# A graph-attention layer on one Trainium2 core: the setup phase reordered, with a second DMA queue on GpSimd

## What is computed

```python
# x [8192, 256], adj [8192, 8192] of zeros and ones, context [8192, 512], W_common [256, 512]
in_fts = context @ W_common.T
left  = in_fts @ w_left  + b_left
right = in_fts @ w_right + b_right
logits = left[:, None] + right[None, :]
logits = where(logits >= 0, logits, 0.2 * logits)
logits = where(adj <= 0, -inf, logits)
out = layernorm(x + relu(softmax(logits, axis=-1) @ x))
```

## Time and profile before

| | us |
|---|---|
| median of 3 runs | 1517.51 (1517.49 to 1521.56) |
| the profiled execution, time | 1518.96 |
| its span in the trace | 1517.2 |
| TensorE busy | 1385.1 (91%) |
| VectorE busy | 1317.8 (87%) |
| ScalarE busy | 645.2 (43%) |
| GpSimd busy | 88.8 (6%) |
| DMA | 329.59 MB, 217 GB/s on average |

### The profile page before, as it was taken

The page is one execution under the profiler, slowest core; times in us unless marked ns, Lnnn a source line. Parts: engine busy times, 40 slices in busy tenths (PEclk is TensorE's granted clock), DMA queues, the critical chain, the costliest instruction groups (busy, mean ns, idle before and its releaser), DMA issues.

```text
span 1517.2 us, 28376 instructions
## 1 busy us (share of the span) xinstructions
PE 1385.1 (91%) x12334; PEld 1207.3 (80%) x12334; DVE 1317.8 (87%) x1178; ACT 645.2 (43%) x690; POOL 88.8 (6%) x214
## 2 busy tenths in 40 slices
PE   1007699999999999999999999999999999999998
PEld 0005588888888888888888888888888888888887
DVE  6759899988998999989998989899998989899881
ACT  0194444443444444443444444344444444444430
POOL 0033000000000000000000000000000000000000
PEclk7558899999999999999999999999999999999999
DMA  9972998989889898989888898989889888988860
GB/s 386 336 167 78 224 234 210 241 213 233 218 220 224 209 230 211 239 215 232 220 218 223 213 225 214 233 220 233 220 219 226 212 225 215 231 217 219 209 168 11
DMA packets 86544, 329.59 MB, mean 217 GB/s; under 512 B 19728, under 2 KB 44304, under 8 KB 52624
## 3 DMA queue, kind: packets, MB, share of 16 engines
q1 hardware_dynamic: 81776, 321.47, 82.8%
q10 hardware_dynamic: 4640, 6.29, 1.5%
HBM read 319.29 MB, written 8.39 MB: 216 GB/s over the span
## 4 chain that ended last, share of the span: by engine, by line
PE 89%; DVE 4%; SPq 3%; DMA 2%; ACT 1%; issue 0%; POOL 0%; POOLq 0%; DVEq 0%
PE ps L352 30%; PE ps L349 30%; PE ps L350 29%; SPq L213 3%; DVE X L615 2%; DMA T<-in_x_dram 2%; DVE strip L652 1%; DVE T L696 1%; DVE tab L518 1%; DMA strip<-in_adj_dram 0%; PE ps L316 0%; ACT strip L423 0%; DMA wcol<-in_L_gnn_w_left_dram 0%; ACT X L394 0%; ACT gw L389 0%
## 5 line engine op out<-in xcount | busy, mean ns | idle before, releaser
L349 PE MATMUL ps<-X,T 128*128 128x257 f16 x4096 | 1117.5, 273 | 38.5 <-DVE T L696 38.4
L350 PE MATMUL ps<-X,T 128*128 128x257 f16 x4096 | 1114.6, 273 | 0.0
L352 PE MATMUL ps<-X,T 128*128 128x257 f16 x4032 | 1107.6, 275 | 0.0
L423 ACT ACTIVATE strip<-strip 128x2048 f32<-128x2048 f32 x256 | 489.2, 1911 | 505.7 <-DMA strip<-in_adj_dram 505.4
L696 DVE STREAM_TRANSPOSE T<-strip 128x2048 f32<-128x2048 f32 x256 | 588.8, 2301 | 74.3 <-PE ps L352 74.3
L652 DVE SCALAR_TENSOR_TENSOR strip<-tab,arow,strip 128x2048 f32<-128x2048 f32 x256 | 597.9, 2336 | 51.5 <-ACT strip L423 50.8
L349 PEld LDWEIGHTS ps<-X,T 128*128 128x128 f16 x4096 | 405.6, 99 | 91.9 <-issue 21.1
L350 PEld LDWEIGHTS ps<-X,T 128*128 128x128 f16 x4096 | 399.9, 98 | 60.8
L352 PEld LDWEIGHTS ps<-X,T 128*128 128x128 f16 x4032 | 391.1, 97 | 54.7
L404 ACT ACTIVATE xs<-ps,small 128x256 f32<-128x256 f32 x64 | 30.3, 473 | 158.2 <-DVE small L701 158.2
L304 POOL TENSOR_SCALAR small<-small 128x1 f32<-128x1 f32 x64 | 12.2, 190 | 1311.6 <-ACT xs L412 1311.6
(11 more groups left out here) (96 smaller groups left out, 250.7 us busy)
## 6 DMA issues: line engine op xcount, KB each, us to landing
strip<-in_adj_dram SPq DMA_DIRECT2D x1016, 256.0 KB, 4.7
xs<-in_L_gnn_context_dram SPq DMA_DIRECT2D x15, 1024.0 KB, 9.7
T<-in_L_gnn_context_dram SPq DMA_DIRECT2D x4, 2048.0 KB, 16.7
X<-in_L_gnn_context_dram SPq DMA_DIRECT2D x4, 2048.0 KB, 34.1
xs<-in_x_dram SPq DMA_DIRECT2D x64, 128.0 KB, 5.1
out_dram<-xs SPq DMA_DIRECT2D x64, 128.0 KB, 5.1
xs<-in_x_dram SPq DMA_DIRECT2D x4, 512.0 KB, 27.8
xs<-in_x_dram ACTq DMA_DIRECT2D x4, 512.0 KB, 20.0
```

Of the source, the lines that this page charges most:

```text
L349: nc.tensor.matmul(ps[o][:, 0:D + 1], hi, X16[:, jb, 0:D + 1], start=(i == 0), stop=False)
L350: nc.tensor.matmul(ps[o][:, 0:D + 1], lo, X16[:, jb, 0:D + 1], start=False, stop=False)
L352: m = nc.tensor.matmul(ps[o][:, 0:D + 1], hi, X16[:, jb, D + 2:2 * D + 3], start=False, stop=(i == JB - 1))
L423: nc.scalar.activation(s, s, ACT.Relu, scale=KEEP).then_inc(s_m, 1)
```

## The change

1. **Second queue.** ScalarE issues no DMA any more. GpSimd issues quarters 2 and 3 of strips 0 to 3 and of x, with semaphores of their own (`s_adjp`, `s_xq`), once the seventh context chunk has landed. SyncE issues quarters 0 and 1 of strips 0 to 3 ahead of those of x, and behind x the context rows of the second `left` block, into `gw`, where the first block's rows lay; the sums of squares write their unused result to PSUM in place of `gw`.
2. **Group 0 ahead of x.** ScalarE takes `keep` of strips 0 to 3, then the sums of squares. VectorE masks and transposes strips 0 to 3, and only then, at n = 4, runs the ones column and `x_factors`.
3. **Halves of x.** Blocks are taken from 63 down to 0. `NPL` is 12: 52 low parts are VectorE's, 13 ahead of each of `masked(4)` to `masked(7)`, and GpSimd makes its 12 (three pairs of operations) after VectorE's 52. ScalarE makes 13 high parts ahead of each of `keep(4)` to `keep(7)`, and the last 12 behind `keep(7)`.
4. **Around group 1.** `masked(8)` comes behind the transpose of strip 7. SyncE waits for the low parts behind the load of strip 11 in place of strip 7.
5. **Shorter chain to the tables.** The operations that prepared the general (wide-spread) case leave the path; the bias add is folded into scalars; ScalarE runs one exponential on a zero at the start.
6. **left steps.** Two operations fewer for each of 15 blocks.

```diff
@@ sync
-            sp.wait_ge(s_dot, 2 * CT)
-            for c in range(NX):
-                for q in (0, 1):
-                    x_quarter(sp, c, q)
             sp.wait_ge(s_v, 2)
             for n in range(NB):
                 for q in (0, 1):
                     strip_quarter(sp, n, q)
+            sp.wait_ge(s_dot, 2 * CT)
+            for c in range(NX):
+                for q in (0, 1):
+                    x_quarter(sp, c, q, s_x[c])
+            sp.wait_ge(s_ld, LB)
+            load_left_rows(1)
...
-                if n == NB - 1:
+                if n == 2 * NB - 1:
                     sp.wait_ge(s_xl, JB - NPL)
                     sp.wait_ge(s_xp, NPL)
-                    load_left_rows(1)
@@ gpsimd
+            pool.wait_ge(s_ctx[NCH - 2], 16)
+            pool.wait_ge(s_v, 2)
+            for n in range(NB):
+                for q in (2, 3):
+                    strip_quarter(nc.gpsimd, n, q, s_adjp[n])
+            pool.wait_ge(s_dot, 2 * CT)
+            for c in range(NX):
+                for q in (2, 3):
+                    x_quarter(nc.gpsimd, c, q, s_xq[c])
             pool.wait_ge(s_Fx, 1)
+            pool.wait_ge(s_xl, JB - NPL)
@@ scalar
-            act.wait_ge(s_ctx[NCH - 3], 16)
-            act.wait_ge(s_dot, 2 * CT)
-            for c in range(NX):
-                for q in (2, 3):
-                    x_quarter(nc.scalar, c, q)
-            act.wait_ge(s_v, 2)
-            for n in range(NB):
-                for q in (2, 3):
-                    strip_quarter(nc.scalar, n, q)
-            act.wait_ge(s_arg, 3)
+            act.wait_ge(s_one, 3)
+            nc.scalar.activation(warm, zero, ACT.Exp)
+            act.wait_ge(s_arg, 2)
...
             with act.If(general == 0):
+                for n in range(NB):
+                    keep(n)
                 for c in range(NX):
                     square_sums(c)
-                for n in range(NB):
-                    keep(n)
-                    for j in order[n * 6:n * 6 + 6]:
-                        high_part(j)
-                for j in order[NB * 6:JB // 2]:
-                    high_part(j)
...
+                    if n < 2 * NB:
+                        for j in order[(n - NB) * 13:(n - NB + 1) * 13]:
+                            high_part(j)
                     keep(n)
-                    if n < 2 * NB:
-                        for j in order[JB // 2 + (n - NB) * 8:JB // 2 + (n - NB + 1) * 8]:
+                    if n == 2 * NB - 1:
+                        for j in order[NB * 13:JB]:
                             high_part(j)
@@ vector
             with dve.If(general == 0):
-                x_factors()
                 masked(0)
                 for n in range(NS):
...
-                    if n + 1 < NS and not SG - 1 <= n < 2 * SG - 1:
+                    if n + 1 < NS and not SG - 1 <= n < 2 * SG:
                         masked(n + 1)
                     if n == SG:
+                        one_columns()
+                        x_factors()
                         dve.wait_ge(s_Fx, 1)
-                        part = (JB - NPL) // SG
                         for i in range(SG):
-                            for j in range(NPL + i * part, NPL + (i + 1) * part):
+                            for j in order[i * 13:(i + 1) * 13]:
                                 low_part(j)
                             masked(n + i)
                         dve.wait_ge(s_xl, JB - NPL)
                     transposed(n, n % NB, g, g % 2, k)
+                    if n == 2 * SG - 1:
+                        masked(n + 1)
```

More of the change, by code:

```diff
@@ L47, in build @@
     LW = LB * SG
-    NPL = 28
+    NPL = 12
     NHI = 2
@@ L117, in xrows @@
             return rows if n > 1 else rows.rearrange("p j d -> p (j d)")
[L119 to L122, removed]
+        order = list(range(JB - 1, -1, -1))
         when = {j: i for i, j in enumerate(order)}
         mx2, ssx = small[:, 0:2], small[:, 2:3]
-        rmin = small[:, 3:4]
         amx = small[:, 4:7]
-        spread, flag, flagf, fast, gscale, cap = (small[:, c:c + 1] for c in range(8, 14))
+        cap, flag, zero, warm = (small[:, c:c + 1] for c in range(8, 12))
         pe2, sc = small[:, 14:15], small[:, 15:16]
@@ L185, in build @@
         s_adj = [sem(f"adj_in{b}") for b in range(NB)]
+        s_adjp = [sem(f"adj_by_pool_in{b}") for b in range(NB)]
+        s_xq = [sem(f"x_by_pool_in{c}") for c in range(NX)]
         s_m = sem("mask_or_exponentials_ready")
@@ L477, in _ @@
                 general_steps(1)
-                with act.Fori(2, NG // NY - 1) as it:
+                with act.Fori(2, NG // NY) as it:
                     general_steps(it)
-                general_steps(NG // NY - 1, more=False)
             for g in range(NG - 2, NG):
@@ L578, in _, with table @@
-            dve.wait_ge(s_word, 6)
-            nc.vector.scalar_tensor_tensor(out=word[:, :], in0=word[:, :], scalar=fast, in1=gen[:, :],
-                                           op0=ALU.mult, op1=ALU.add).then_inc(s_word, 1)
-            dve.wait_ge(s_word, 7)
-            nc.vector.transpose(tab[:, :].rearrange("p (c j) -> p j c", c=B),
-                                word[:, 0:JB].rearrange("p (j c) -> p j c", c=1).broadcast_to([P, JB, B])).then_inc(s_tab, 1)
+            def table():
+                nc.vector.transpose(tab[:, :].rearrange("p (c j) -> p j c", c=B),
+                                    word[:, 0:JB].rearrange("p (j c) -> p j c", c=1).broadcast_to([P, JB, B])).then_inc(
+                    s_tab, 1)
@@ L593, in x_factors, with second_left_dots @@
+            def second_left_dots():
+                dve.wait_ge(s_lc, 32)
+                for q in range(LB):
+                    left_dot(1, q, lctx01, Xflat[:, q % 2 * CIN:(q % 2 + 1) * CIN])
+                    if q < LB - 1:
+                        dve.wait_ge(s_ld, LB + q)
+                left_by_strip(1)
             def x_factors():
@@ L616, in low_part, with general_tables, left_step @@
                                                in1=X16[:, j, 0:D], op0=ALU.mult, op1=ALU.subtract).then_inc(s_xl, 1)
-            def left_step(b, k):
+            def general_tables():
+                nc.vector.memset(F[:, :], 1.0).then_inc(s_gt, 1)
+                nc.vector.tensor_scalar(word[:, 0:JB], r[:, :], rmax, -1.0 / BIG, ALU.subtract, ALU.mult).then_inc(s_gt, 1)
+                dve.wait_ge(s_amx, 6)
+                nc.vector.tensor_scalar(arow[:, 0:LW], pt[:, 0:LW], c2, None, ALU.add).then_inc(s_gt, 1)
+                dve.wait_ge(s_gt, 3)
+                table()
+                dve.wait_ge(s_tab, 3)
+            def left_step(b, k, fast=True):
+                if not fast and isinstance(b, int) and b == 1 and k <= 11:
+                    return
                 if 7 <= k < 7 + LB:
@@ L623, in left_step @@
                     dve.wait_ge(s_ld, b * LB + q - 1)
-                    left_dot(b, q, lctx, ljunk[:, q % 2, :])
+                    left_dot(b, q, lctx01 if isinstance(b, int) and b == 1 else lctx, ljunk[:, q % 2, :])
                 if k == 11:
@@ L748, in _ @@
             with dve.Else():
+                second_left_dots()
+                general_tables()
+                one_columns()
                 x_factors()
                 dve.wait_ge(s_Fx, 1)
-                for j in range(NPL, JB):
+                for j in order[0:JB - NPL]:
                     low_part(j)
```

164 lines of the change are left out of this document (82 added, 82 removed).

## The result

| | before | after |
|---|---|---|
| median of 6 runs each, us | 1518.77 | 1512.16 (1510.99 to 1514.82) |
| the profiled execution's span, us | 1517.2 | 1509.6 |
| TensorE busy | 1385.1 | 1390.0 |
| first high part, H | 92.6 | 109.3 |
| group 1 starts | 163.3 | 152.1 |

The ratio is 0.9955 (95% interval 0.9945 to 0.9965): faster by 0.45%, some 7 us, where 23.3 us (to 1494.2) was forecast. The sign was right, the size off by a factor of more than three, and the time lies above the stated range, which ended at 1508.

What follows compares the result with a forecast made beforehand. TensorE's waits for VectorE's transposes before group 2 were taken as the bound. H at 96.5 plus 66.2 starts group 2 at 162.7 against 186.0, 23.3 us off, giving a median of 1494.2 us; range 1486 to 1508.

Steps and rivals of the forecast that it cites:

- When is H: End of setup: x lands at 91.6, two sums of squares follow, first high part at 96.5, 3.9 us later than before.
- both move at 348 GB/s while two queues run: Setup loads from about 52 us: SyncE's and GpSimd's queues together move x and strips at 348 GB/s.
- rivals 3 and 4: Setup: GpSimd issues at 10 to 15 ns a packet, 1499 to 1517, chance 0.12; 17 to 20 ns, 1526 to 1540, 0.08.
- GpSimd's last quarter of x by 92: Setup, sign to look for in GpSimd's queue: its last x quarter lands by 92 us.
- the 236 GB/s of the earlier trace: Setup loads: rate taken for one queue left alone, against 348 GB/s for two.
- The sums of squares: Setup on ScalarE: 16 of 1.18 us, 19 us from 67, ready at 86 and then waiting for x.
- Tables and group 0: Setup: table transpose near 63, strips 0 to 3 masked and transposed from 65 to 83, all covered by x's arrival.
- The ladder from H to group 1: First high part to group 1: transposes 4 to 7 end at H+40.6, GpSimd at H+42.4, group 1 starts at H+43.
- Group 2: Behind group 1: VectorE's transpose of strip 11 sets the start, H+66.2 = 162.7, against 186.0 before.
- The sum: Whole kernel: group 2 starts 23.3 us sooner, span 1517.2 becomes 1493.9, median forecast 1494.2 us.
- the rivals: Setup and feed: x sooner, 1486 to 1490, chance 0.18; later feed, 1499 to 1506, 0.15; slower GpSimd, 0.12 and 0.08.

Runs made afterwards that it cites:

- e9: Changed kernel with six of the 16 sums of squares moved from ScalarE to VectorE; 1510.86 us, ratio 0.9941.
- e10: e6 with six of the 16 sums of squares moved from ScalarE to VectorE; 1500.84 us, ratio 0.9870.
- e6: Changed kernel with SyncE's quarters of x read in 4 KB pieces in place of 1 KB; 1505.88 us, ratio 0.9910.
- e7: Changed kernel with GpSimd issuing only its strip quarters, and ScalarE issuing quarters 2 and 3 of x in portions between its work; 1509.67 us, ratio 0.9940.
- e8: e7 with ScalarE's last x transfers issued earlier and six of the 16 sums of squares on VectorE; 1501.00 us, ratio 0.9878.
- e1: Changed kernel with GpSimd's 18 transfers issued by ScalarE behind the same waits; 1510.39 us, ratio 0.9934.
- e3: Changed kernel with SyncE's quarters of x read in pieces of 8 to 16 KB in place of 1 KB; 1518.47 us, ratio 0.9987.

## Why the prediction was wrong

**When is H: wrong, and the main miss.** The failing step is "both move at 348 GB/s while two queues run". I took the pace of ScalarE's queue for GpSimd's, and asked of it only how fast it issues. It issues fast: 18 transfers in 10.3 us, from 43.7 to 54.0, while VectorE's dot products ran without a gap (busy 10.0 of the 10 us from 44 to 54), so rivals 3 and 4, with their ns a packet and the dot products that shut GpSimd out, were about the wrong quantity. The sign that I had named, GpSimd's last quarter of x by 92, came true (no packet of its queue moves after 90), and H was late all the same: it was SyncE's half that starved. What changed is the packet: 4640 for 6.29 MB became 1568 for the same bytes. Turns by packet then starve SyncE. Landing of the last chunk: 91.6 forecast, 105.1 in e9, 93.7 with packets alike (e10). The Trainium skill says it in "DMA: Bandwidth & Descriptors", "Queues, rings and completion order": each engine goes round between the queues a packet at a time. The traces bear this rule out: equal packet counts wherever both queues had work throughout the window. I weighed the same page for who writes the descriptors, and passed over this rule. I had also misread the 236 GB/s of the earlier trace rows as one queue left alone; it was two queues, SyncE's at 224 packets and ScalarE's at 77, which ran to 85 and not to 73.

**The sums of squares: wrong, hidden behind the first miss.** "Ready at 86 and wait for x" had the first chunk at 67. It lands at 74.5 to 78.7 even with like packets (e6, e7, e8, e10), and 19 us of sums stand behind it. In the changed kernel dividing the sums is worth 0 (e9); with like packets 2.4 to 5.8 us (e6 to e10, above).

**Tables and group 0: right.** Tables near 63 and at 62.2; strips from 65 to 83 in both. All of it lies ahead of the last sum of squares, at 107, so it delays nothing; what it gains is that these strips no longer stand in the ladder.

**The ladder from H to group 1: right to 0.2 us.** Forecast and trace: low parts 0.40 each; `masked(7)` H+31.7 and H+31.6; transposes H+40.6 and H+40.5; GpSimd H+42.4 and H+42.3; group 1 H+43 and H+42.8, at full clock.

**Group 2: right in kind, small in size.** Forecast H+66.2, started at H+67.7, and the low clock behind a wait of 3.2 us added the other 1.4: 2.9 us in all (1400.3 from H to the end, against 1397.4 forecast). What waited was not the first matmul of group 2 but the matmul of the left factors ahead of it; I had named VectorE's lateness and not priced the clock.

**The sum.** 12.8 us at H and 2.9 behind it are all of the 15.7 us by which 1509.6 exceeds 1493.9. Of the 12.8, like packets and divided sums together give back 11.2 (e10). The other 1.6 was not tested. One thing that the forecast had wrong is of this size: the strips moved at 282 GB/s and not at 348, although their packets were alike (129 and 127, 0.71 and 0.70 MB, over 55 to 60 in the changed kernel); for 4.2 MB that is 2.8 us, an estimate from these two rates. None of the rivals held this mechanism: each was about how early x comes when both queues keep their pace, how fast GpSimd issues, or the feed behind H.

## What to carry to other kernels

When a transfer changes queue, compare what its packets will be with those of its neighbour: bytes are shared by packet size, and the smaller one is starved until the larger is done. Read it from the trace as packets and MB of each queue in one window; equal counts with unequal bytes are the sign. And when the last arrival is what counts, work out the first arrival as well, since the work on what arrives queues up behind it; an early gain at one group is only kept if the next group's inputs keep pace.

## What the runs showed of the hardware

- In windows of 5 us in which both had work throughout, two queues had equal packet counts (284 and 283, 877 and 877, 99 and 100, 224 and 222, 302 and 305), whatever their sizes: 1 KB for rows of 1 KB from SyncE or ScalarE, about 3.6 KB for the same rows from GpSimd.
- Two queues with like packets, on different quarters of the partitions, moved x at 348 GB/s (1 KB) and 326 (about 3.6 KB); with unlike ones, 240 to 272; SyncE alone with 1 KB rows, 195 to 200. Strips, with 5.5 KB a packet on both queues, moved at 282.
- GpSimd's issue of 18 transfers took 10.3 us; ScalarE's of the same took 35.8 (e1).
- A stretch of 3.2 us at a granted clock of 0.51 (16 matmuls) followed the wait ahead of group 2 where that was 2.9 to 3.7 us (the changed kernel, e1, e3, e10), and not where it was 1.2 to 1.9 (e6 to e9); but in these last the same stretch had come at group 1, behind a wait of 2.0 to 2.4, so the length of the wait is not shown to be what decides.
- A sum of squares of 1024 columns takes VectorE 1.23 us (1.26 with its read) with both operands in SBUF, ScalarE 1.18 with its read.
